# A frame pipeline on one core: the order of ScalarE, VectorE and GpSimd within a frame is written anew, with three result buffers and no buffer of its own for the transposed weights

## What is computed

```
row_zero  = x.sum(-1) == 0                       # rows whose sum is zero get no query
self_feat = [x, where(row_zero, 0, q)] @ W_self.T + b_self          # (512, 512)
out = self_feat
for d in (0, 1):
    A    = mask[:, :20, :] or its transpose       # (512, 20, 11)
    cond = A.sum(-1);   vb = A @ w_bias + b_bias
    kv   = self_feat[:20]
    aff  = heads(self_feat @ Wq[d].T + bq[d]) . heads(kv @ Wk[d].T + bk[d]) / sqrt(32)   # 16 heads
    w    = softmax(where(cond > 0, aff, -9e15) + vb)
    out += per head (w @ kv) @ Wout[d] + bout[d]
result = x + relu(out)
```

## Time and profile before

| | us |
|---|---|
| median of three runs | 643.92 |
| the profiled execution | 643.25 |
| its span, first to last instruction | 641.5 |
| TensorE matmul busy in the span | 597.1 |
| GpSimd busy | 449.4 |
| VectorE busy | 439.8 |
| ScalarE busy | 415.1 |
| mean granted TensorE clock | 0.989 of full speed |

### The profile page before, as it was taken

How to read it: one execution, slowest core, us unless ns; L and a number is a source line. 1 busy time by engine, 2 the same in 40 slices (tenths; PEclk the granted TensorE clock), 3 DMA queues, 4 the chain that set the end, 5 groups by cost and what they waited for, 6 DMA issues and landing times.

```text
span 641.5 us, 11259 instructions
## 1 busy us (share of the span) xinstructions
PE 597.1 (93%) x4303; PEld 500.0 (78%) x4303; DVE 439.8 (69%) x638; ACT 415.1 (65%) x829; POOL 449.4 (70%) x400
## 2 busy tenths in 40 slices
PE   9999999899898989989898998989899999999895
PEld 6977888688686878868686886968687787888682
DVE  4896696577575766766677675757876666677475
ACT  5666758775766777474868666576875666773342
POOL 0402497955979786697977579797659798875973
PEclk9999999989999999999998999999999999999998
DMA  8975344653757564384655367474617656573234
GB/s 317 413 292 145 71 136 160 157 179 82 226 138 201 144 198 148 72 277 102 234 120 192 107 145 229 106 248 111 211 56 182 190 144 216 135 208 80 95 57 147
DMA packets 43395, 106.96 MB, mean 167 GB/s; under 512 B 12494, under 2 KB 26830, under 8 KB 36942
## 3 DMA queue, kind: packets, MB, share of 16 engines
q1 hardware_dynamic: 41182, 90.51, 43.0%
q0 software_dynamic: 2160, 15.73, 13.3%
HBM read 86.74 MB, written 19.47 MB: 166 GB/s over the span
## 4 chain that ended last, share of the span: by engine, by line
PE 35%; POOL 26%; ACT 18%; DVE 13%; issue 4%; DMA 3%; SPq 1%; DVEq 0%; POOLq 0%
POOL xl L1235 10%; PE aff L567 10%; POOL z L1254 8%; PE aff L537 6%; ACT sff L754 5%; ACT xn L714 4%; PE tp L581 3%; ACT prod L728 3%; DVE cond L1000 3%; POOL z L1266 3%; PE gen L498 3%; PE gen L499 2%; PE gen L500 2%; DVE z L1006 2%; POOL sff L1277 2%
## 5 line engine op out<-in xcount | busy, mean ns | idle before, releaser
L498 PE MATMUL gen<-xh,w1h 128*128 128x512 f32 x256 | 106.3, 415 | 14.4 <-DVE sff L953 14.4
L567 PE MATMUL aff<-gh,sfh 128*128 128x320 f32 x504 | 117.7, 315 | 0.0
L567 PE MATMUL aff<-gh,sfl 128*128 128x320 f32 x504 | 114.8, 309 | 0.0
L567 PE MATMUL aff<-gl,sfh 128*128 128x320 f32 x504 | 114.8, 309 | 0.0
L1242 POOL TENSOR_TENSOR z<-cb,bx 128x640 f32<-128x640 f32 x64 | 102.7, 1637 | 10.2 <-PE tp L500 10.2
L1254 POOL TENSOR_TENSOR z<-z,mx 128x640 f32<-128x640 f32 x63 | 85.2, 1353 | 25.8 <-DVE mx L1008 25.7
L499 PE MATMUL gen<-xl,w1h 128*128 128x512 f32 x256 | 102.0, 398 | 0.0
L1235 POOL TENSOR_TENSOR xl<-x,xh 128x512 fp32r<-128x512 f32 x62 | 84.7, 1597 | 24.7 <-ACT xh L708 24.7
L500 PE MATMUL gen<-xh,w1l 128*128 128x512 f32 x256 | 101.7, 397 | 0.0
L1021 DVE TENSOR_REDUCE rcp<-z 128x32 f32<-128x640 f32 x64 | 52.1, 814 | 61.5 <-ACT z L886 61.5
L567 PEld LDWEIGHTS aff<-gh,sfh 128*128 128x128 f32 x504 | 83.2, 188 | 13.1 <-issue 12.6
(11 more groups left out here) (158 smaller groups left out, 1112.7 us busy)
## 6 DMA issues: line engine op xcount, KB each, us to landing
x<-in_x SPq DMA_DIRECT2D x16, 1024.0 KB, 7.7
xn<-in_xn SPq DMA_DIRECT2D x31, 512.0 KB, 4.7
sff<-in_x POOLq DMA_DIRECT2D x15, 1024.0 KB, 8.2
out_y<-sff SPq DMA_DIRECT2D x15, 1024.0 KB, 4.0
msk<-in_mask SPq DMA_DIRECT2D x17, 880.0 KB, 5.9
cb<-c_scratch SPq DMA_DIRECT2D x16, 320.0 KB, 5.6
nz<-nz_scratch SPq DMA_DIRECT2D x16, 256.0 KB, 3.4
wkT<-in_wkT SPq DMA_DIRECT2D x4, 512.0 KB, 8.0
```

The costliest lines, as they stand in the source:

```text
L498: nc.tensor.matmul(acc, lh, rh, start=first, stop=False)
L567: mm = nc.tensor.matmul(aff[:, t % 2, half, 0:SH], s, g[:, b - starts[group(b)], f, half * SH:(half + 1) * SH], start=(f == 0 and i == 0), ...
```

## The change

What it does:

- `add_x(b)` and the store of frame b are issued during frame b + 1: on GpSimd `add_x(b - 1)` comes after `value_rest(b)`, on SyncE `store_out(b - 1)` comes after the mask. `sff` has three buffers for this, used by b % 3.
- `wt` is gone. The transposed weights are evicted into `zr` (chunk 0) and into the slot of `z` that they came from (chunks 1 to 4). GpSimd therefore waits for the attention products of b - 1 before it writes `zr` again (`s_pv`).
- ScalarE computes the labels of frame n = b + 1 in frame b, not those of b + 2; the mask of b + 2 is loaded after the labels of n. Its exponential 3 comes before the first `evict_g`.
- The row sums of b + 2 are made by VectorE, in two halves, after `total(b, 3)` and after the label sums. The second half needs the second load into `xn`, which SyncE issues after the first half's sum.
- VectorE takes `x_low` of block 3 over from GpSimd in every frame. The label sums move from the start of its frame to behind `add_query(n, 2)`, `label_mask` to behind `sf_low`.
- TensorE's score tile 0 waits for the last `g_low` only at its last block.

Its core (a third of the lines are renames of `sff[slot]` to `sff[b % 3]`; what is removed stands in the listing above):

```diff
-wt = sb("wt", [P, WC, N])
+sff.append(sb("sff2", [P, FC, N]))
...
+def wt(b, c):
+    return zr[:] if c == 0 else z[b % 2][:, :, (c - 1) * P:c * P]
...
+    return (s_xl, FC + XP + (n - 2) * (FC - 1) + c + 1) if c < FC - 1 else (s_xl1, XP + n - 1)
...
+    def store_out(b):
+        sp.wait_ge(s_ya, b * 16 + 16)
+        sp.dma_start(out[bass.ds(b, 1)].rearrange("o p c n -> p (o c n)"),
+                     sff[b % 3][:].rearrange("p c n -> p (c n)")).then_inc(s_out[b % 3], 16)
...
-        if ahead == 2:
-            sp.wait_ge(s_rsum, b * 2 + 5)
-            load_rows(b + 2, 1)
         if ahead >= 1:
             sp.wait_ge(s_bx, b * T + T)
             load_c(b + 1)
         if ahead == 2:
-            sp.wait_ge(s_xl, x_lows(b + 1, FC - 1))
+            for c in (FC - 2, FC - 1):
+                sp.wait_ge(*x_lows(b + 1, c))
             if b == 0:
-                sp.wait_ge(s_xl1, FC - XP)
+                sp.wait_ge(*x_lows(1, XP - 1))
             load_x(b + 2)
-            sp.wait_ge(s_neg, b * 3 + 9)
-            load_mask(b + 3)
+            sp.wait_ge(s_rsum, b * 2 + 5)
+            load_rows(b + 2, 1)
+            if b > 0:
+                sp.wait_ge(s_prod, (b + 2) * LG)
+                load_mask(b + 2)
+        if b > 0:
+            store_out(b - 1)
+        if ahead == 2:
             store_nonzero(b + 2)
             load_rows(b + 3, 0)
...
-            sp.wait_ge(s_ya, b * 16 + 16)
-            sp.dma_start(out[bass.ds(b, 1)].rearrange("o p c n -> p (o c n)"),
-                         sff[slot][:].rearrange("p c n -> p (c n)")).then_inc(s_out[slot], 16)
...
+                if t == 0 and f == 0:
+                    pe.wait_ge(s_gl, pair * GU + GU - 1)
+                elif t == 0 and f == FC - 1:
+                    pe.wait_ge(s_gl, pair * GU + GU)
...
-    def row_sums(n, half, count):
...
         act.wait_ge(s_tp, last_tp(c) if b == B - 1 else chunk(b, c + 1))
-        nc.scalar.activation(wt[:, c, :], wt_bank(b, c), ACT.Copy).then_inc(s_wt, 1)
+        if b == B - 1 and c == LAST_ORDER[0]:
+            act.wait_ge(s_wr, b * T + T)
+        nc.scalar.activation(wt(b, c), wt_bank(b, c).rearrange("p (t q) -> p t q", t=T), ACT.Copy).then_inc(s_wt, 1)
...
+    def next_labels(n, k):
+        if k == 0:
+            act.wait_ge(s_mskin, n * 16 + 16)
+            act.wait_ge(s_vred, n * D)
+        labels(n, range(k, L, LG))
     def batch(b, slot, i, ahead):
         n, other = b + 1, 1 - slot
         next_g, pair = next_group(b) is not None, next_group(b)
...
+            exponential(0, 0, 0)
...
+        elif ahead >= 1 and b > 0:
+            next_labels(n, 0)
...
+        exponential(b, slot, 1)
+        if ahead >= 1 and b > 0:
+            next_labels(n, 0 if next_g else 1)
+        exponential(b, slot, 2)
+        if ahead >= 1 and b > 0:
+            next_labels(n, 1 if next_g else 2)
+        exponential(b, slot, 3)
+        if next_g:
+            evict_g(pair, 0)
+            evict_g(pair, 1)
+            sf_high(n, other, 0)
+            if b > 0:
+                next_labels(n, 2)
+                edge_terms(n)
+            sf_high(n, other, 1)
+            evict_g(pair, 2)
+            evict_g(pair, 3)
+            sf_high(n, other, 2)
+            evict_g(pair, 4)
+            evict_g(pair, 5)
+        else:
+            if b > 0:
+                edge_terms(n)
+            for f in range(FC - 1):
+                sf_high(n, other, f)
...
+        exponential(n, other, 0)
...
+            if n >= 3:
+                dve.wait_ge(s_out[n % 3], n // 3 * 16)
...
         shift(b, slot, 3)
+        add_query(n, other, 0)
+        total(b, slot, 2)
+        total(b, slot, 3)
+        dve.wait_ge(s_nzc, b + 2)
+        row_sums(b + 2, 0, xn[:], s_xnin, b * 32 + 48)
         dve.wait_ge(s_bx, T)
         label_sum(n, 0)
         label_sum(n, 1)
-        dve.wait_ge(s_out[other], 16)
-        add_query(n, other, 0)
-        total(b, slot, 2)
-        total(b, slot, 3)
+        row_sums(b + 2, 1, xn[:], s_xnin, b * 32 + 64)
         add_query(n, other, 1)
+        add_query(n, other, 2)
         label_mask(n + 1)
-        add_query(n, other, 2)
...
+        total(b, slot, 0)
+        shift(b, slot, 1)
         if ahead >= 1:
-            dve.wait_ge(s_bx, b * T + T)
+            x_low(n, FC - 1)
         shift(b, slot, 2)
         total(b, slot, 1)
...
         shift(b, slot, 3)
         total(b, slot, 2)
-        dve.wait_ge(s_out[other], (i + slot) * 16 + 16)
         add_query(n, other, 0)
+        total(b, slot, 3)
+        if ahead == 2:
+            dve.wait_ge(s_nzc, b + 2)
+            row_sums(b + 2, 0, xn[:], s_xnin, b * 32 + 48)
         if next_g:
             g_low(pair, 0)
             g_low(pair, 1)
         add_query(n, other, 1)
         if next_g:
             g_low(pair, 2)
             g_low(pair, 3)
+        add_query(n, other, 2)
+        dve.wait_ge(s_bx, b * T + T)
+        label_sum(n, 0)
+        label_sum(n, 1)
+        if next_g:
             g_low(pair, 4)
             g_low(pair, 5)
-        else:
-            add_query(n, other, 2)
+        if ahead == 2:
+            row_sums(b + 2, 1, xn[:], s_xnin, b * 32 + 64)
+        if next_g:
+            g_low(pair, 6)
+        add_query(n, other, FC - 1)
+        if next_g:
+            g_low(pair, 7)
+        sf_low(n, other)
         if ahead == 2:
+            label_mask(b + 2)
         shift(n, other, 0)
         for j in range(HG):
...
-    def add_x(b, slot):
...
+                x_low(n, 0)
+                x_low(n, 1)
+            pool.wait_ge(s_pv, b * HG)
             normalise_rest(b, slot, 0)
             normalise(b, slot, 0)
+            sub_max(b, slot, 1)
+            if ahead >= 1:
+                x_low(n, 2)
         sub_max(b, slot, 2)
         normalise_rest(b, slot, 1)
...
+        value_rest(b)
+        if b > 0:
+            add_x(b - 1)
         if ahead >= 1:
             for f in range(FC - FL):
...
-            add_x(b, slot)
...
```

More of the change, by code:

```diff
@@ L390, in batch @@
                             sp.wait_ge(s_y3, j)
-                        sp.dma_start(out[b, :, j], sff[slot][:, j, :]).then_inc(s_out[slot], 16)
-                    sp.wait_ge(s_out[0], (B // 2) * 16 + 16)
-                    sp.wait_ge(s_out[1], (B // 2 - 1) * 16 + HG * 16 + 16)
+                        sp.dma_start(out[b, :, j], sff[b % 3][:, j, :]).then_inc(s_out[b % 3], 16)
+                    for k in range(3):
+                        stored = len(range(k, B, 3))
+                        sp.wait_ge(s_out[k], (stored - 1 + HG if k == b % 3 else stored) * 16)
             batches(batch)
@@ L614, in start_sum @@
                 pe.wait_ge(s_bs, j + 1)
-                nc.tensor.matmul(pv_bank(b, j), ident[:], sff[slot][:, j, :], start=True, stop=False)
+                nc.tensor.matmul(pv_bank(b, j), ident[:], sff[b % 3][:, j, :], start=True, stop=False)
             def attend_rest(b, slot):
@@ L909, in batch @@
                     return
-                if ahead == 2:
-                    row_sums(b + 2, 1, b * 32 + 64)
+                exponential(b, slot, 3)
[17 more added lines that the diff above has]
+                        sf_high(n, other, f)
                 evict_wt(b, 0)
                 evict_wt(b, 1)
-                if b == 0:
-                    labels(2, range(1, L, LG))
-                    sf_high(1, 1, 2)
                 if next_g:
@@ L923, in batch @@
                 evict_wt(b, 4)
-                if b == 0:
-                    labels(2, range(2, L, LG))
-                    edge_terms(2)
                 if ahead == 2:
@@ L1205, in batch @@
                     g_low(pair, 1)
-                total(b, slot, 3)
                 add_query(n, other, 1)
-                if ahead == 2:
-                    label_mask(b + 2)
                 if next_g:
@@ L1305, in batch @@
                     if ahead >= 1:
-                        for c in range(FC):
-                            x_low(n, c)
-                    sub_max(b, slot, 1)
+                        x_low(n, 0)
+                        x_low(n, 1)
+                    pool.wait_ge(s_pv, b * HG)
                     normalise_rest(b, slot, 0)
                     normalise(b, slot, 0)
+                    sub_max(b, slot, 1)
+                    if ahead >= 1:
+                        x_low(n, 2)
                 sub_max(b, slot, 2)
                 normalise_rest(b, slot, 1)
-                if b > 0:
-                    value_rest(b)
                 normalise(b, slot, 1)
```

118 lines of the change are left out of this document (36 added, 82 removed).

## The result

The changed kernel takes 645.5 us (median of 13 runs, 644.8 to 649.7); the kernel before took 644.0 beside it (13 runs, 641.3 to 647.3). The ratio is 1.0043, 95% interval 1.0026 to 1.0061: a little slower, where 612 was forecast and 603 to 631 given as the range. The profiled execution has a span of 643.8 us.

What follows compares the result with a forecast made beforehand. GpSimd's loop sets the period, TensorE only follows. 641.5 less 25.1 (plain frames), 2.3 (frame 14) and 14.0 (group frames), plus 6.5 (frame 0) and 3.3 (tail): span 609.9, forecast 612, range 603 to 631.

Steps and rivals of the forecast that it cites:

- What bounds the kernel: Plain frames: the loop through GpSimd sets the 33.3 us period and TensorE, with a floor of 30.08, only follows.
- The order laid end to end: Plain frames walked in time from score tile 1: all three TensorE waits go, 33.29 to 30.15 us each, 25.1 over eight.
- the slack of 1.0: Plain frame, score tile 0: it wants VectorE's sf_low at 27.0 us and has it at 26.0.
- the paragraph on the port: VectorE and GpSimd: x_low beside sub_max(b, 1) may cost either side up to 1.3 us per frame, one loss hidden by slack.
- Frame 0: First frame: product 3 waits for add_query(1, 1) behind both row sums, 96.0 to 101.1; 6.5 us lost, bounds 3.5 and 9.
- Group frames: Five frames of 39.1 us each, 195.5 in place of 209.5, with two g_low 0.2 to 0.3 late: 14.0 us saved.
- rival D: Group frames gain little: g_low late enough for the clock to fall again, 42 us each, 626.5 in all; chance 0.12.
- The tail: End of the kernel: last stores issue behind the late add_x(14) and its landing; 3.3 us lost, bounds 2 and 5.
- B: Another engine's order becomes the bound: VectorE or GpSimd loses 1.3 us per frame, 18 over 14 frames, 630; chance 0.14.
- E: Late second half of the rows delays sf_low, so score tile 0 waits in every frame; 679 at 12 us landing; chance 0.04.
- F: The loop closes elsewhere (s_pv, prod) with the old period and only the edges change: 654 us; chance 0.03.

Runs made afterwards that it cites:

- the first experiment: The changed kernel with GpSimd's add_x(b - 1) issued right behind sub_max(b, 1) instead of behind value_rest(b): 608.75 us, ratio 0.9454 to the kernel before.

## Why the prediction was wrong

- *What bounds the kernel* was right. The loop through GpSimd held a plain frame at 33.3 us: with it opened and the shut-out removed the frame is 29.8, TensorE's busy time, a little under the 30.08 I took as its floor.
- *The order laid end to end* held in all but one number. In frame 5 `sf_low` starts 24.6 us after score tile 1 (24.7 in the walk), and TensorE asks for it at 26.8 (27.0 in the walk). But I gave it 1.3 us and it took 4.73. The walk itself says what follows: 3.4 us more, less the slack of 1.0, is a wait of 2.4; 2.65 was measured, in nine frames (23.8 us). With the lower clock that came with it in six of them it makes the 28.8 and the 4.0 above.
- *The step that failed is the paragraph on the port.* It looked for a meeting at the place where the change put a new VectorE instruction (x_low beside sub_max) and allowed one loss of 1.3 us. It did not look at the old meeting of `sf_low` with the bias, whose cost the change alters by moving a DMA issue ahead of it. The new meeting cost little (`x_low` on VectorE has a median of 0.72 us). I cost the move of `add_x` by its ReLU wait, its landing and its store, not by what follows it on GpSimd. The Trainium skill (page "SBUF — State Buffer", section "Who interferes with whom") says that whoever issues first holds the shared ports for its whole instruction while the other engine is blocked; by that a shut-out lasts one instruction. Where GpSimd had idled behind its DMA issue the traces agree (`nonzero` 1.54 us beside one bias of 2.03 in frame 5 of the first experiment). Behind an issue without idle they do not: VectorE was kept out for the rest of the four, 4.73 us, and over all of four, 6.63.
- *Frame 0* was right: forecast a wait from 96.0 to 101.1 and 6.5 us lost; measured 5.26 us up to 101.67, a granted clock of 0.50 from 101.6 to 104.0 behind it, and 6.5 us.
- *Group frames* were right within 0.5 us, and rival D was wrong; the 0.2 to 0.3 us by which two `g_low` were to come late did not show.
- *The tail* was mis-sized: 3.3 forecast, 6.6 measured. `add_x(14)` went out 1.9 us before TensorE's last attention product, not the 3.0 of my figures; it took 8.8 us to land, not 8.2; and the four last stores took 3.84 us to issue, not the 2.0 of the earlier trace rows.
- *Rivals.* B named the port but priced it at one GpSimd instruction and 18 us. E named the very wait that came, for `sfl` in score tile 0, but by a late load; in the changed kernel the load was in time, and E's mechanism showed only in the variants. (E's 679 is a span; with the 1.75 around it, it would be some 681.) What came, plain frames near their old length while frame 0 and the tail lost 13 us, comes nearest to F, for another reason: the loop through GpSimd did open, and what held the plain frames was the shut-out.

## What to carry to other kernels

A DMA that GpSimd issues has a cost beyond its issue time: look at which GpSimd instructions follow it with no idle between, and which VectorE instruction falls into that run, however small it is: in these runs it was a 128x512 subtraction and a 128x4 comparison. When a change moves such an issue, walk that run anew, instructions that did not move included. Where GpSimd waits several times anyway, put the issue just ahead of such a wait; the wait must still be unmet when GpSimd comes to it.

## What was unexpected

- Behind a GpSimd-issued DMA, of 1 MB or of 64 bytes, four bias instructions kept VectorE out until the last had ended: `sf_low` 4.73 us in place of 1.35, `nonzero` 6.63 in place of 0.17. With idle time between the issue and the bias they did not (`sf_low` 0.70 to 1.38 us in the plain frames of the first experiment), and an idle of 0.15 us was enough. GpSimd's rows overlapped behind the 1 MB issue and not behind the 64 bytes, though both kept VectorE out. What inside GpSimd does this no run shows.
- A wait of 2.65 us of TensorE did not always cost the clock: frames 2, 5 and 8 stayed at 1.00 and six others fell to 0.92 to 0.95 with the same wait (32.7 against 34.2 to 34.9 us).
